# Re-ordering one round of a 16-round attention pipeline on four engines

## The reference

```python
qkv = silu(hidden @ qkv_w.T)               # 32 heads of 128: q, k, v
scores = einsum('bhnd,bhmd->bhnm', q, k) * decay   # causal, blockwise with a carried state
attn = scores @ v                          # linear attention, no softmax
xf = attn * rsqrt(mean(attn * attn) + 1e-5)
gate = sigmoid(hidden @ gate_w.T)
return (gate * norm_w * xf) @ out_w.T
```

## Time and profile before

| | us |
|---|---|
| median of 3 runs | 2735.97 |
| lowest, highest | 2733.24, 2742.16 |
| profiled execution, its own time | 2737.41 |
| its span, first to last instruction | 2735.6 |
| TensorE busy (matmuls) | 2531.7 (93%) |
| TensorE's weight loads | 2163.1 (79%) |
| GpSimd busy | 1543.1 (56%) |
| VectorE busy | 1509.4 (55%) |
| ScalarE busy | 1351.3 (49%) |
| mean granted clock of TensorE | 0.969 |

### The profile page before, as it was taken

How to read it: one execution, slowest core, us unless ns; L and a number is a source line. 1 busy time by engine, 2 the same in 40 slices (tenths; PEclk the granted TensorE clock), 3 DMA queues, 4 the chain that set the end, 5 groups by cost and what they waited for, 6 DMA issues and landing times.

```text
span 2735.6 us, 42276 instructions
## 1 busy us (share of the span) xinstructions
PE 2531.7 (93%) x13850; PEld 2163.1 (79%) x13850; DVE 1509.4 (55%) x2449; ACT 1351.3 (49%) x2694; POOL 1543.1 (56%) x1523
## 2 busy tenths in 40 slices
PE   7999999999999899989999999999999989968999
PEld 6778888787878788777878787888878778857777
DVE  6554545545464545874454545545454678865553
ACT  5445554555554544544545454545455547743332
POOL 4655656565565754756576666666666558831110
PEclk9999999999999999999999999999999999989999
DMA  4210111111111112311111101111111148941100
GB/s 152 78 47 28 58 38 46 50 36 48 42 50 35 54 40 67 106 43 43 43 42 42 58 27 58 46 38 50 35 50 43 37 151 300 303 158 35 47 31 31
DMA packets 89052, 183.87 MB, mean 67 GB/s; under 512 B 12610, under 2 KB 38866, under 8 KB 88966
## 3 DMA queue, kind: packets, MB, share of 16 engines
q1 hardware_dynamic: 80422, 165.94, 18.4%
q0 software_dynamic: 8544, 16.82, 2.1%
HBM read 163.81 MB, written 26.79 MB: 70 GB/s over the span
## 4 chain that ended last, share of the span: by engine, by line
PE 45%; issue 18%; POOL 16%; DVE 9%; ACT 8%; DMA 2%; POOLq 0%; ACTq 0%; DVEq 0%; SPq 0%
PE bank L95 14%; PE bank L96 14%; PE bank L97 14%; POOL wl L1924 5%; POOL sqacc L1942 2%; POOL w_in L508 2%; POOL w_in L512 2%; POOL w_in L510 2%; DVE el L2322 2%; POOL w_in L514 2%; POOL ol L1936 2%; ACT wh L1383 1%; ACT sq L1368 1%; PE bank L1115 1%; DVE ms_lo L1665 1%
## 5 line engine op out<-in xcount | busy, mean ns | idle before, releaser
L1924 POOL TENSOR_TENSOR wl<-w_in,wh 128x512 fp32r<-128x512 f32 x510 | 602.6, 1204 | 339.2 <-ACT wh L1383 334.6
L95 PE MATMUL bank<-xh,wh 128*128 128x512 f32 x1400 | 575.2, 411 | 8.4 <-ACT bank L1331 6.3
L97 PE MATMUL bank<-xh,wl 128*128 128x512 f32 x1400 | 557.2, 398 | 0.0
L1383 ACT CAST wh<-w_in 128x512 fp32r<-128x512 f32 x502 | 263.8, 568 | 319.5 <-POOL w_in L514 319.5
L1942 POOL TENSOR_TENSOR sqacc<-sqacc,sq 128x512 f32<-128x512 f32 x128 | 167.5, 1308 | 400.4 <-ACT sq L1368 387.9
L96 PE MATMUL bank<-xl_sums,wh 128*128 128x512 f32 x800 | 320.3, 400 | 0.0
L97 PEld LDWEIGHTS bank<-xh,wl 128*128 128x128 f32 x1400 | 269.7, 193 | 61.2
L95 PEld LDWEIGHTS bank<-xh,wh 128*128 128x128 f32 x1400 | 270.9, 193 | 58.8 <-ACT bank L1331 7.2
L1708 DVE TENSOR_TENSOR acc<-bank,acc 128x512 f32<-128x512 f32 x240 | 165.1, 688 | 233.8 <-PE bank L97 233.7
L95 PE MATMUL bank<-wh,xh 128*128 128x256 f32 x912 | 258.7, 284 | 4.4 <-DVE xl L566 3.3
L95 PE MATMUL bank<-oh,yh 128*128 128x512 f32 x512 | 209.0, 408 | 56.3 <-DVE acc L1708 52.3
(11 more groups left out here) (373 smaller groups left out, 6381.0 us busy)
## 6 DMA issues: line engine op xcount, KB each, us to landing
w_in<-in_w_pairs_dram SPq DMA_DIRECT2D x100, 512.0 KB, 3.8
o_in<-in_o_pairs_dram SPq DMA_DIRECT2D x32, 512.0 KB, 4.9
eraw<-in_ex_dram SPq DMA_DIRECT2D x31, 513.0 KB, 4.9
y_slots<-ey SPq DMA_DIRECT2D x31, 512.0 KB, 5.9
w_in<-in_w_pairs_dram SPq DMA_DIRECT2D x56, 256.0 KB, 3.0
dcur<-in_decay_dram SPq DMA_DIRECT2D x32, 256.0 KB, 3.0
eraw<-in_ex_dram SPq DMA_DIRECT2D x31, 256.0 KB, 5.4
out_dram<-acc SPq DMA_DIRECT2D x16, 256.0 KB, 2.0
```

The source lines that it names most:

```text
L95: pe.matmul(out, wh, mh, start=start and i == 0, stop=False, skip_group_check=True)
L97: ins = pe.matmul(out, wl, mh, start=False, stop=stop and i == n - 1, skip_group_check=True)
L1383: a.copy(wh[:, cols], w_in[:, cols]).then_inc(w_hi, 1)
L1924: pool.tensor_tensor(wl[:, cols], w_in[:, cols], wh[:, cols].bitcast(F32), ALU.subtract).then_inc(w_lo, 1)
```

## The change

The groups of attention are spread otherwise over the round's products. The table of groups is named anew (the same heads and sequences). The pieces of two groups now lie side by side in the bank `sc[1]`, so `pieces` of groups 0 and 1 of the next unit both run in the round before. `scores(0)`, its masks, the low parts of scores, of values and of the keys and queries of group 1 are done in the round before as well. In even rounds the split of the output weights goes before that of g, on ScalarE and on GpSimd. `values` of group 2 and 3 and the output products move later. The load of `o_in` waits for the eighth output product. In the diff below, lines of the new orders that belong together stand on one line, and the removed orders are those told above.

```diff
-ITEMS = ((0, 0), (0, 1), (1, 0), (1, 1), (0, 2), (0, 3), (1, 2), (1, 3))
+GROUP_OF = ((0, 0), (1, 0), (0, 2), (1, 2))
+PIECE_N, SCORE_N = (1, 2, 5, 7), (3, 4, 6, 8)
-             "even": {"g": 4, "o": 6, "v0": 10, ...
+             "even": {"o": 2, "g": 6, "v0": 10, ...
-    READY = {..., "even": (-4, 0, 4, 14), ...
+    READY = {..., "even": (-4, 0, 6, 14), ...
 # SP
+                    if not r.first:
+                        wait(sp, pe_out, 8 * r.u + 8)
                     sp.dma_start(o_in[:], o_pairs[n]).then_inc(dma_o, 16)
 # TensorE, pieces
-                    if r is None or not r.first:
+                    if g >= 2:
                         wait(pe, v_mask, u * 8 + (2 * g - 1))
                     for i in range(2):
-                        c = slice((b + i) * S + P, (b + i + 1) * S)
-                        ins = pe.matmul(sc[1][:, i * P:(i + 1) * P], ...
+                        c, to = slice((b + i) * S + P, (b + i + 1) * S), (g % 2) * 2 + i
+                        ins = pe.matmul(sc[1][:, to * P:(to + 1) * P], ...
 # TensorE, a round that is not the first (new order)
+                        section(r, 0, 1)
+                        values(r, 0)
+                        scores(r.u, 1)
+                        section(r, 0, 5)
+                        pieces(r.u, 2)
+                        section(r, 0, 6, 2, 7, 3)
+                        values(r, 1)
+                        scores(r.u, 2)
+                        section(r, 0, 4)
+                        section(r, 1, 1)
+                        pieces(r.u, 3)
+                        section(r, 1, 5)
+                        project_out(r, 0)
+                        section(r, 1, 6)
+                        values(r, 2)
+                        scores(r.u, 3)
+                        project_out(r, 1)
+                        section(r, 1, 2)
+                        project_out(r, 2)
+                        section(r, 1, 7)
+                        project_out(r, 3)
+                        section(r, 1, 3)
+                        if r.end:
+                            values(r, 3)
+                        section(r, 1, 4)
...
+                        section(r, 2, 1)
+                        values(r, 3)
+                        pieces(r.n, 0, r)
+                        pieces(r.n, 1)
+                        section(r, 2, 5, 6)
+                        scores(r.n, 0)
+                        section(r, 2, 2, 7)
+                        project_out(r, 4)
+                        section(r, 2, 3)
+                        project_out(r, 5)
+                        section(r, 2, 4)
+                        project_out(r, 6)
+                        project_out(r, 7)
 # ScalarE, begin of the round (new order)
+                    take(r, 0, "ab")
+                    square(u, 0); y_high(u, 0)
+                    take(r, 0, "t5")
+                    high_ms(u, 1); high_v(u, 1, odd, r.takes); high_kq(u, 2)
+                    split_o(u, 0); split_o(u, 1)
+                    if r.even: split(r, "g", 0, 1)
+                    take(r, 0, "a")
+                    if r.even: split(r, "g", 2, 3)
+                    square(u, 1)
+                    take(r, 0, "e"); take(r, 0, "c")
+                    y_high(u, 1); high_ms(u, 2); high_v(u, 2, odd)
+                    take(r, 0, "b"); take(r, 1, "ab"); take(r, 1, "t5")
+                    high_kq(u, 3)
...
 # ScalarE, section 2
+                    square(u, 3); y_high(u, 3)      # after take(r, 2, "ab")
+                    take(r, 2, "a"); high_ms(r.n, 0)
+                    if r.odd: high_v(r.n, 0, ...); high_kq(r.n, 1)
 # VectorE (new order)
+                        gated(u, 0); mask_pieces(u, 1); mask(u, 1); y_low(u, 0); low_ms(u, 1)
+                        summed(r, 0, "c"); low_v(u, 1, odd); low_kq(u, 2); summed(r, 0, "e")
+                        gated(u, 1); mask_pieces(u, 2); mask(u, 2); y_low(u, 1)
+                        low_ms(u, 2); low_v(u, 2, odd); add_out(u, 0); low_kq(u, 3); summed(r, 1, "c")
+                        gated(u, 2); mask_pieces(u, 3); mask(u, 3); low_ms(u, 3); low_v(u, 3, odd)
+                        add_out(u, 1); add_out(u, 2); summed(r, 1, "e"); add_out(u, 3); y_low(u, 2)
+                        gated(u, 3); low_kq(n, 0); mask_pieces(n, 0); y_low(u, 3)
...
+                        norm_weights(n); summed(r, 2, "c"); mask(n, 0); summed(r, 2, "e"); low_ms(n, 0)
+                        if r.odd: low_v(n, 0, True); low_kq(n, 1)
+                        for t in range(TPG, HTILES): add_out(u, t)
 # GpSimd
-                    if r.even:
-                        add_low(r, "g")
-                        add_squares(u, 1)
-                        low_o(r)
-                    else:
-                        add_squares(u, 1)
-                        low_o(r)
-                        add_low(r, "g")
+                    low_o(r)
+                    add(r, "g")
+                    add_squares(u, 1)
+                    low(r, "g")
...
-                        add_low(r, "v0")
+                        add(r, "v0")          # its low part now after add_squares(u, 2)
```

More of the change, by code:

```diff
@@ L1101, in values @@
                     u = r.u
[L1102 to L1104 removed]
+                    if g or not zero(u):
                         wait(pe, a_sq, 4 * u + g)
@@ L1442, in run @@
                             split(FRONT[h], "v", 0, 1)
-                    if not r.first:
-                        high_v(r, 0)
-                        high_ms(u, 0)
-                        high_kq(u, 1)
+                    odd = r.even or r.end
                     take(r, 0, "ab")
-                    take(r, 0, "t5")
                     if r.first:
+                        take(r, 0, "t5")
                         blocks[h].take_route(a, 0, sc[0])
@@ L1459, in run @@
                         y_high(u, 0)
-                        high_v(r, 1)
+                        take(r, 0, "t5")
                         high_ms(u, 1)
+                        high_v(u, 1, odd, r.takes)
                         high_kq(u, 2)
+                        split_o(u, 0)
+                        split_o(u, 1)
                     if r.even:
@@ L1500, in run @@
                         split_o(UNITS, 1)
-                    if not r.first:
-                        square(u, 2)
-                        high_v(r, 3)
-                        high_ms(u, 3)
                     take(r, 1, "t5")
@@ L1537, in run @@
                     if r.second or r.odd:
-                        split(r, "q", 0, 1)
+                        split(r, "q", 0)
                     take(r, 2, "ab")
+                    if not r.first:
+                        square(u, 3)
+                        y_high(u, 3)
                     if r.first:
@@ L1557, in run @@
                     take(r, 2, "a")
+                    if not r.first:
+                        high_ms(r.n, 0)
+                    if r.odd:
+                        high_v(r.n, 0, True, r.takes)
+                        high_kq(r.n, 1)
+                    take(r, 2, "e")
+                    take(r, 2, "c")
+                    if r.second or r.odd:
+                        split(r, "k", 0, 1)
+                    if r.even:
+                        split(r, "v1", 3)
+                    take(r, 2, "b")
                     if r.second or r.odd:
                         split(r, "k", 2, 3)
-                    take(r, 2, "e")
-                    take(r, 2, "c")
-                    take(r, 2, "b")
                     if r.first:
@@ L1736, in run @@
                     n, u, first, second, end = r.n, r.u, r.first, r.second, r.end
+                    odd = r.even or end
                     if first:
@@ L1784, in run @@
                         mask(u, 2)
-                        y_low(u, 1)
-                        low_v(r, 2)
-                        low_ms(u, 2)
-                        low_kq(u, 3)
-                        if second and last:
-                            router.place(v, slot_of, v_slots)
                         if end:
@@ L1793, in run @@
                             shared_product(0, 0)
+                        y_low(u, 1)
+                        low_ms(u, 2)
+                        low_v(u, 2, odd)
+                        if second and last:
+                            router.place(v, slot_of, v_slots)
+                        add_out(u, 0)
+                        low_kq(u, 3)
+                        summed(r, 1, "c")
                         gated(u, 2)
@@ L1817, in run @@
                         gated(u, 3)
+                        if not end:
+                            low_kq(n, 0)
+                            mask_pieces(n, 0)
                         y_low(u, 3)
```

197 lines of the change are left out of this document (94 added, 103 removed).

## The result

The changed kernel takes **2633.51 us** (median of 4 runs, 2630.56 to 2635.34), against 2734.60 (4 runs, 2731.98 to 2742.16) for the kernel before on the same chip: ratio 0.9625, 95% interval 0.9603 to 0.9646. The forecast was 2636 us. The profiled execution took 2634.02, its span is 2632.2 (before: 2735.6).

The account below looks back on a forecast made before the run. TensorE's idle gaps, mainly waits on VectorE, and the slow clock they bring were the cost. Pairs of 118.8 + 3.3 + 1.3 = 123.4 us save 106; with second rounds, rounded to 105, less 5: 2636 us, range 2595 to 2690.

Parts of the forecast that it names:

- the 5 us taken off for unplaced waits: Whole kernel: the rounded gain of 105 us was cut by 5 for lesser waits not placed, leaving 100.
- The floor: A pair of even and odd round: TensorE's work alone takes 69.7 and 49.1, together 118.8 us, unchanged by the change.
- The even round: Even rounds: TensorE still stands 1.6 us before section 1, then 0.5, 0.2 and 1.0; together 3.3 us.
- The odd round: Odd rounds: 0.8 us lost at `scores(3)` for `q_lo`, 0.5 at `project_out(6)` in the tail; 1.3 in the sum.
- The rule weighed: Odd tail: if GpSimd blocks each of VectorE's four low parts, they take about 7 us instead of 4.3.
- Rival A: Odd tail: four low parts at 6.3 us make `project_out(6)` 2.4 late, 3.6 more per odd round; 2686 us, chance 0.13.
- Rival B: Even rounds: the clock still falls, from close gaps or stretched sums, adding 24 us; 2660 us, chance 0.20.
- Rival C: Even rounds, ScalarE before g's split: late `o_in` delays TensorE beyond 1.7 us of cover; slower, example 2790 us, chance 0.06.
- Rival D: VectorE as late in other places, so the bound stays; time within 8 us of before, chance 0.03.
- Rival E: Even rounds: `split_o` and the sums come early enough, 35 us more gained; 2601 us, chance 0.13.
- Second rounds: Second rounds lose a 3.13 us gap and its slow clock (about 5), 3.5 comes back; net gain 1.5 twice.
- End rounds: End rounds: bounded by plus or minus 3 us each, taken as 0, since additions are moved, not removed.

Follow-up runs that it names:

- e1: The kernel before with one edit on VectorE: `add_out(0)` moved ahead of `low_v(3)`; 2679.99 us, ratio 0.9799.
- e9: The changed kernel with one part undone: `add_out(0)` again behind `low_v(3)` on VectorE; 2670.22 us, ratio 0.9737.
- e2: The kernel before, GpSimd writing low parts of g and output weights in even rounds as zeros but for 8 columns of each piece; 2707.28 us.
- e3: The changed kernel with ScalarE's four casts of g in even rounds moved behind `high_v(2)` and `high_kq(3)`; 2562.21 us, ratio 0.9378.
- e11: The changed kernel with g's casts later, `low_kq(3)` before `add_out(0)`, router spread, first-tail k splits later, end-round `low_o` earlier; 2549.41 us, ratio 0.9292.
- e10: The changed kernel with the `low_ms(n, 0)` subtraction made twice on VectorE in the odd rounds' tail; 2639.3 us, ratio 0.9623.
- e12: The changed kernel with SP issuing even rounds' `o_in` only behind section 0's second product, 4.6 us later; 2645.19 us, ratio 0.9656.
- e6: The changed kernel with the router's VectorE work spread over idle times in the second half's second round; 2630.70 us, ratio 0.9624.
- e7: The changed kernel, GpSimd writing low parts of g and output weights in even rounds as zeros but for 8 columns; 2587.56 us.

## Why the prediction was right, and where it was wrong

The mechanism was right: the odd round's stop hung on the place of `add_out(0)` (e1, e9), the even round's gaps of the first half on ScalarE's and GpSimd's work on g and o (two of three go in e2), and the new stop stands where it was forecast (e3). How near the number came is in part luck. The pair came out at 123.7 against 123.4, of terms that were off in opposite directions. The pairs gave 100.7 us where 105.7 were forecast, and the 5 us taken off for unplaced waits happened to cover that. And the sum has a slip: 106 for the pairs and 3 for the second rounds are 109, not the 105 that was written.

- **The floor** of 118.8: measured 118.5. Right.
- **The even round**, 3.3 forecast, 4.5 measured. The steps were right to a few tenths: ScalarE at `split_o` at 6.96 (6.9), the sums' end at 14.1 (13.5), the stop before section 1 1.77 (1.6). The smaller ones are 0.23 (0.5), 0.49 (0.2) and 0.65 (1.0): 3.14 in all, against 3.3. What failed is the sum: I charged 0.2 of restart, a figure from no row, to each gap of the kernel before and none to those of the forecast. With the same work, TensorE is busy 70.51 us in the round with the stops

```profile
515.04:588.80 73.76, 70.51 (x423) 61.86 (x422) 40.06 (x52) 38.20 (x74) 47.77 (x47) 1.00 0.15 48
```

  and 69.2 in that of e11 without one (379.68 to 448.89; the window here begins 1.3 us late, and is busy throughout):

```profile
381.00:450.30 69.30, 69.30 (x424) 62.03 (x424) 38.22 (x51) 39.27 (x76) 47.19 (x45) 1.00 0.16 49
```

  The difference is 1.3 us for five stops, 0.26 each. Set side by side, the timelines of the two rounds show what it is made of. In a full stream a matmul starts 0.23 us after the one before and so overlaps it by 0.16, which a bracket leaves out; and the second matmul behind a stop starts 0.33 us after the first, 0.1 more than in the stream. The fifth stop, of 0.10 and so 0.36 in all, I had not placed.
- **The odd round**, 1.3 forecast, 0.6 measured. Mid-round 0.28 stands of 0.8. In the tail I took 0.5 for `project_out(6)`: the four low parts began 42.3 us into the round (41.3 taken) and took 4.05 (4.3 taken), the first addition is done as the product is due, and 0.14 is lost. e10 shows that it is just so.
- **The rule weighed**, that the second of the two engines blocks (the Trainium skill, "SBUF — State Buffer", section "Who interferes with whom"): the four took 4.05 us, not the 7 that I had set beside the rule. But the trace agrees with the kind of the rule: each of the four took about 0.5 us longer than alone (1.14, 0.95, 0.96, 1.22 for 0.69, 0.41, 0.41, 0.69), beside sums of GpSimd such as

```profile
507.32 0.74 POOL L511 TENSOR_TENSOR w_in<-w_in 128x256 f32<-128x256 f32 x1
508.14 1.07 POOL L513 TENSOR_TENSOR w_in<-w_in 128x256 f32<-128x256 f32 x1
```

  What was wrong is the size in the 7: 1.1 more for each is what the low parts of 128x512 cost (1.78 for 0.69), and these sums are 0.74 long when nothing meets them.
- **Rival A** (the wait moves to the tail): refuted; no wait there. **Rival B** (the clock still falls): its sign was there in two of the fourteen even rounds: the granted clock is 0.52 from 408.2 to 411.6, behind a gap of 1.77 like those of the other even rounds:

```profile
408.20:411.60 3.40, 3.40 (x12) 2.84 (x11) 1.55 (x2) 3.37 (x8) 3.13 (x3) 0.52 0.05 17
```

  It cost nothing: that round is 73.80 long, the next 73.76, since the waits of 0.23, 0.49 and 0.10 that come next fall away when TensorE runs slower. **Rival C**: the cover was mis-sized, 3.3 us (e12) where I gave 1.7, because `o_in` landed 3.4 us after its issue instead of 5.0. **Rival D** (the bound stays) is out: 101 us were gained. **Rival E** (even rounds do better) did not come; e3 makes the kernel so, by moving four casts of g.
- **Second rounds**, net gain 1.5 each forecast. The first half's got 2.8 us shorter (70.8 to 68.0). In the second half it failed: the round got 5.4 us longer (73.3 to 78.7). The step that failed is "net 1.5 twice": I passed over the router, whose instructions on VectorE now stand ahead of `add_out(0)`, `low_kq(3)` and `summed(1,e)`. They began at 1145.5 and 1157.9 and held `q_lo` and `t` back until the stops of 3.95 and 4.08; e6 and e11, which move them, shorten the round to 76.2 and 71.6.
- **End rounds**, taken as 0: new is 0.86 us for `ol` in each, since GpSimd adds the squares of group 1 before `low_o` (e11, with these two the other way round, has neither). Gone in the last one are waits of 0.70 and 2.35 for `ms_lo` and `acc`, a net gain of 2.2; and behind the 2.35 the granted clock had been 0.56 for 3.6 us (2196.0 to 2199.6 of the kernel before), which is 1.6 more.

What stays open: some 1.6 of the 5.4 us by which the part after the pairs is shorter; in e7, what the engines' meeting costs apart from GpSimd's own length; and what the parts of the new order (the pieces and `scores(0)` a round earlier, the later values and output products) are worth one by one, as no run undoes them singly.

## What to carry to other kernels

When two engines pass work in a circle, look for the instruction that stands ahead of a take in a queue although nothing waits for it yet: two casts, 1.14 us together, stood there here and waited 6 us for a third engine, and moving them, with the two behind the take, gave 4.6 us a round. A new gap costs more than its bracket (0.26 us each here), and a gap taken away uncovers the one that it hid, so value parts of a change by undoing them in the new order as well as by doing them in the old. And work that occurs once in the program (the router) shares the queue that was rearranged for the common round: follow its round separately.

## What the runs showed of the hardware

- VectorE's small instructions are stretched the most beside GpSimd's subtractions of 128x512, in proportion: 0.18 us for 128x32 became 1.2 (changed kernel, 1148.20); 0.41 for 128x256 became 1.51; 0.69 for 128x512 became 1.22 to 1.78. Written as zeros (e2), GpSimd's low parts leave them at 0.41 and 0.68.
- A delay can take part of itself back by ending a meeting: in e12 ScalarE came 1.31 us later and TensorE's wait grew by 0.7, in e10 an added 1.15 us moved the addition by 0.6.
- A fall of the granted clock to the 1.2 GHz level cost nothing where the other engines were late anyway (73.80 us against 73.76). In the kernel before it did cost: the even round of 75.55 is 6.3 above the 69.2 without a stop, its three stops of 3.63 in all and 0.26 for each make 4.4, and the rest, 1.9, is about the 1.7 of the slow stretch.
